# Layers 1 and 2 of a recommendation tower's MLP for two tiles at once, behind TensorE's inner loop

## The reference, cut to what matters

```python
x1 = einsum('bik,bjk,hij->bhk', e, e, W1) + b1      # e: [2048, 26, 32], gathered by ids
x2 = einsum('bik,bjk,hij->bhk', x1, e, W2) + b2     # 128 outputs each
z = concat([x1, x2], axis=1).sum(-1)                # [2048, 256]
h = concat([z, dense_ctx], axis=1)                  # [2048, 272]
h = maximum(h @ W_top1 + b_top1, 0)                 # "layer 1", 512 wide
h = maximum(h @ W_top2 + b_top2, 0)                 # "layer 2", 256 wide
y = h @ W_top3                                      # [2048, 1]
```

## Time and profile before

| | us |
|---|---|
| median of 3 runs | 509.12 (507.92 to 512.33) |
| the profiled execution | 510.54 |
| its span | 508.7 |
| mean granted TensorE clock | 0.993 |

### The profile page before, as it was taken

How to read it: one execution, slowest core, us unless ns; L and a number is a source line. 1 busy time by engine, 2 the same in 40 slices (tenths; PEclk the granted TensorE clock), 3 DMA queues, 4 the chain that set the end, 5 groups by cost and what they waited for, 6 DMA issues and landing times.

```text
span 508.7 us, 25085 instructions
## 1 busy us (share of the span) xinstructions
PE 479.8 (94%) x10786; PEld 461.8 (91%) x10786; DVE 377.7 (74%) x1095; ACT 253.5 (50%) x530; POOL 348.9 (69%) x274
## 2 busy tenths in 40 slices
PE   4998889969699999999999999999999999999998
PEld 4887879869699999999999999999999999999997
DVE  8698949495778788797969597959695968773202
ACT  8866835364525463636364545454454545455111
POOL 5888977467887888787878787878787887700000
PEclk9999999989989999999999999999999999999999
DMA  6620022120111102020202020202020200000000
GB/s 216 171 95 13 15 56 47 28 60 13 37 40 30 44 16 53 13 59 10 59 12 58 13 58 13 57 13 59 11 59 12 59 10 12 9 1 3 1 1 1
DMA packets 14001, 19.57 MB, mean 38 GB/s; under 512 B 5123, under 2 KB 11528, under 8 KB 13838
## 3 DMA queue, kind: packets, MB, share of 16 engines
q0 software_dynamic: 8512, 4.38, 8.1%
q1 hardware_dynamic: 5454, 14.73, 8.0%
HBM read 19.08 MB, written 0.01 MB: 38 GB/s over the span
## 4 chain that ended last, share of the span: by engine, by line
PE 78%; DVE 8%; issue 3%; ACT 3%; DMA 3%; POOL 2%; SPq 1%; ACTq 0%; DVEq 0%; POOLq 0%
PE psum L927 21%; PE psum L901 18%; PE psum L946 12%; PE psum L972 8%; PE psum L880 7%; PE psum L994 4%; PE psum L922 4%; DVE work L631 3%; POOL emb L389 2%; DMA onehot<-in_tbl 2%; PE psum L967 2%; DVE onehot L479 2%; DMA emb<-in_tbl,idx 1%; ACT t_area L742 1%; ACT v L706 1%
## 5 line engine op out<-in xcount | busy, mean ns | idle before, releaser
L389 POOL DMA_INDIRECT emb<-in_tbl,idx x266 | 348.1, 1309 | 95.0 <-issue 63.5
L742 ACT COPY t_area<-psum 128x432 f32<-128x432 f32 x256 | 124.5, 543 | 98.2 <-PE psum L901 71.3
L631 DVE TENSOR_TENSOR work<-embT 128x32 f32<-128x32 f32 (+12 forms) x416 | 129.3, 386 | 0.0
L927 PE MATMUL psum<-t_area,v 128*128 (+1 forms) x1088 | 124.1, 275 | 0.0
L927 PEld LDWEIGHTS psum<-t_area,v 128*128 128x128 f32 x1088 | 122.8, 192 | 0.0
L901 PE MATMUL psum<-diag,work 64*64 64x54 f32 (+1 forms) x6144 | 102.1, 216 | 4.8 <-ACT t_area L742 2.0
L901 PEld LDWEIGHTS psum<-diag,work 64*64 64x64 f32 (+1 forms) x6144 | 93.3, 126 | 11.5 <-issue 6.0
L719 ACT COPY diag<-embT 32x416 f32<-32x416 f32 x128 | 69.9, 546 | 20.6 <-DVE embT L613 19.1
L946 PE MATMUL psum<-table_parts,onehot 125*128 125x96 bf16 x1350 | 63.7, 208 | 4.1 <-DVE onehot L479 2.4
L946 PEld LDWEIGHTS psum<-table_parts,onehot 125*128 125x128 bf16 x1350 | 59.4, 99 | 6.5 <-DVE onehot L479 2.7
L880 PE MATMUL psum<-diag,work 128*64 128x108 f32 (+1 forms) x1024 | 51.5, 262 | 8.5 <-DVE work L631 6.6
(11 more groups left out here) (96 smaller groups left out, 447.1 us busy)
## 6 DMA issues: line engine op xcount, KB each, us to landing
ids_all<-in_short_ids SPq DMA_DIRECT2D x15, 625.0 KB
emb<-in_tbl,idx POOLq DMA_INDIRECT x266
t_area<-in_L_rec_W SPq DMA_DIRECT2D x1, 1664.0 KB, 8.5
work<-in_W_top SPq DMA_DIRECT2D x2, 512.0 KB, 12.2
onehot<-in_tbl SPq DMA_DIRECT2D x5, 156.2 KB
onehot<-in_tbl SPq DMA_DIRECT2D x5, 125.0 KB
t_area<-in_L_rec_W SPq DMA_DIRECT2D x1, 338.0 KB, 4.0
idx<-in_ids SPq DMA_DIRECT2D x1, 208.0 KB, 2.5
```

Of the source, the lines that this page charges most:

```text
L389: eng.indirect_dma_start(emb[n][:, f * K:(f + 1) * K], None, tables[f], bass.IndirectOffsetOnAxis(ap=idx[:, t * F + f:t * F + f + 1], axis=0),
L631: last = nc.vector.tensor_tensor(pairs[:, half, :, :, tri(r):tri(r) + r + 1], halves[:, g, :, 0:r + 1], halves[:, g, :, r:r + 1].broadcast ...
L742: nc.scalar.copy(dst, src).then_inc(t_out, 1)
L927: last = nc.tensor.matmul(z_ps(t)[:, NP:2 * NP], v[:, s, :], moments(slot), start=(a == 0), stop=(a == len(terms) - 1))
```

## The change

Layers 1 and 2 leave the inner loop's step and stand behind every second step (`layers(pair)`): layer 2 of the two tiles of a pair, then layer 1 of the next pair, for both tiles in one matmul of 256 columns. h1 of the four blocks of 128 outputs needs two PSUM banks then: blocks 0 and 1 are in bank 4, blocks 2 and 3 in bank 7, which rows part 0 and layer 2 of the pair's second tile use as well. ScalarE and VectorE move h1 in two halves per pair, and VectorE does `make_y` for two tiles together. Layer 1 of tiles 0 and 1 stands ahead of the loop. `pair` is i in round i of the loop, whose steps are 2i+3 and 2i+4.

```diff
+        def h2_ps(n):
+            return psum[:, 6 + n, 0:N2]
+        def h1_ps(half):
+            return psum[:, (4, 7)[half], :].rearrange("p (a b) -> p a b", b=2 * NP)
...
         def marks_in(t):
-            layers, cross = t >= 3, t != 1
-            return len(MARK_PHASES) + 2 + 2 * layers + len(MARK_TERMS) * cross
+            layer1, layer2, cross = t >= 2 and t % 2 == 0, t >= 4 and t % 2 == 0, t != 1
+            return len(MARK_PHASES) + 2 + 2 * layer1 + 2 * layer2 + len(MARK_TERMS) * cross
...
         (VectorE, tile)
                 make_pairs(t, n, (lambda: make_onehot(t + 1)) if not known or t + 1 < TILES else None)
                 if not known or t >= 2:
                     z_low(t - 2, n)
-                if not known or t >= 4:
-                    make_y(t - 4)
+                if n == 1 and (not known or t >= 5):
+                    for tile_of_pair in range(2):
+                        make_y(2 * i - 4 + tile_of_pair, tile_of_pair)
                 if not known or t >= 2:
                     pack(t - 1, 1 - n)
-                if not known or t >= 3:
-                    h1_low(t - 3)
+                if n == 1 and (not known or t >= 3):
+                    h1_low(i - 1)
...
         (ScalarE, step)
-                if not known or 3 <= t < TILES:
-                    h1_move(t - 3)
...
                 if not known or t >= 1:
-                    z_move(t - 1, 1 - n)
+                    z_move(t - 1, i - 1 + n, 1 - n)
+                if n == 0 and (not known or t >= 2):
+                    h1_move(i - 1)
...
         (TensorE, short_rows)
                     eng.wait_ge(rows_ready, t - 1)
-                    if part == 1 and not (isinstance(t, int) and t < 5):
-                        eng.wait_ge(y_ready, t - 3)
+                    if pair is not None:
+                        eng.wait_ge(y_ready if part else h1_lo_ready, 2 * pair + (1 if part else 3))
...
+            def layer1(pair):
+                if not (isinstance(pair, int) and pair == TILES // 2 - 1):
+                    eng.wait_ge(rows_ready, 2 * pair + 3)
+                eng.wait_ge(h1_lo_ready, 2 * pair + 1)
+                eng.wait_ge(z_out, 2 * pair + 2)
                 for a in range(N1 // NP):
+                    if a == 2:
+                        eng.wait_ge(y_ready, 2 * pair + 1)
+                    dst = h1_ps(a // 2)[:, a % 2, :]
                     cols = slice(a * NP, (a + 1) * NP)
+                    nc.tensor.matmul(dst, top1d[:, cols], denseT[:, bass.ts(pair, 2 * NP)], start=True, stop=False)
                     for top1, z in ((top1_hi, z_hi), (top1_lo, z_hi), (top1_hi, z_lo)):
                         if a == 0 and z is z_lo:
+                            eng.wait_ge(z_lo_ready, 2 * pair + 2)
...
-                t_units(t, 0)
-                if not known or t >= 3:
-                    layer1(t - 3, n)
-                t_units(t, 1)
-                if not known or t >= 3:
-                    layer2(t - 3)
-                if not known or t >= 2:
+                for half in range(2):
+                    t_units(t, half, pair)
+                if not isinstance(t, int) or t >= 2:
                     cin(t - 1, n)
+            def layers(pair):
+                for n in range(2):
+                    layer2(2 * pair + n, pair, n)
+                layer1(pair + 1)
...
+            layer1(0)
             with eng.Fori(0, (LOOP[1] - LOOP[0]) // 2) as i:
                 with eng.Fori(0, 2) as n:
-                    step(2 * i + n + LOOP[0], n)
+                    step(2 * i + n + LOOP[0], i, n)
+                layers(i)
```

More of the change, by code:

```diff
@@ L751, in z_move, with h1_move @@
                     .then_inc(z_out, 1)
[L753 to L759, removed]
+            def h1_move(pair):
+                if not (isinstance(pair, int) and pair < 1):
+                    eng.wait_ge(h2_full, 2 * pair)
+                for half in range(2):
+                    eng.wait_ge(h1_full, 2 * pair + half + 1)
+                    nc.scalar.activation(h1_hi[:, 2 * half:2 * half + 2, :], h1_ps(half), ACT.Relu).then_inc(h1_out, 1)
             def step(t, i, n):
@@ L792, in _ @@
                 step(t, t // 2, t % 2)
[L793 to L796, removed]
+            z_move(TILES - 1, TILES // 2 - 1, 1)
+            h1_move(TILES // 2 - 1)
         @block.tensor
@@ L861, in t_units @@
                             if v == at:
-                                short_rows(t + 1, part)
+                                short_rows(t + 1, part, pair)
                     if isinstance(t, int):
@@ L931, in cin, with short_rows @@
                 last.then_inc(z_full, 1)
-            def short_rows(t, part):
+            def short_rows(t, part, pair):
                 eng.wait_ge(onehot_ready, t)
@@ L973, in layer1, with layer2 @@
                                                     start=False, stop=(z is z_lo and s == 1))
-                    if a == 2:
-                        last.then_inc(progress, 1)
-                last.then_inc(h1_full, 1)
-            def layer2(t):
-                hi, lo = h1_parts(t)
-                eng.wait_ge(h1_out, t + 1)
-                if isinstance(t, int) and t == TILES - 1:
+                    last.then_inc(h1_full if a % 2 else progress, 1)
+            def layer2(t, pair, n):
+                eng.wait_ge(h1_out, 2 * pair + 2)
+                if isinstance(t, int) and t + 4 >= TILES:
@@ L993, in layer2 @@
                     for s in range(N1 // NP):
-                        last = nc.tensor.matmul(dst, h1[:, s * NP:(s + 1) * NP], top2[:, s, :], start=False,
-                                                stop=(h1 is lo and s == N1 // NP - 1))
-                        if h1 is lo and s == N1 // NP - 2:
+                        last = nc.tensor.matmul(dst, h1[:, s, n * NP:(n + 1) * NP], top2[:, s, :], start=False,
+                                                stop=(h1 is h1_lo and s == N1 // NP - 1))
@@ L997, in layer2, with step @@
+                        if h1 is h1_lo and s == N1 // NP - 2:
                             last.then_inc(progress, 1)
                 last.then_inc(h2_full, 1)
-            def step(t, n):
-                known = isinstance(t, int)
-                t_units(t, 0)
-                if not known or t >= 3:
-                    layer1(t - 3, n)
-                t_units(t, 1)
-                if not known or t >= 3:
-                    layer2(t - 3)
-                if not known or t >= 2:
+            def step(t, pair, n):
+                for half in range(2):
+                    t_units(t, half, pair)
+                if not isinstance(t, int) or t >= 2:
```

83 lines of the change are left out of this document (28 added, 55 removed).

## The result

| | before | after |
|---|---|---|
| median, us | 510.73 (507.92 to 512.87, 4 runs) | 544.87 (541.85 to 552.03, 4 runs) |
| ratio to before | | 1.0652, 95% interval 1.0563 to 1.0742 |
| the profiled execution | 510.54 | 541.85 |
| its span | 508.7 | 540.1 |
| mean granted TensorE clock | 0.993 | 0.949 |

The account below looks back on a forecast made before the run. GpSimd was taken to be as full as TensorE, behind its 94% busy share. Five pairs +26, start +6.2 and end -7.0 us, together +25, took the 508.7 us span to 534; median forecast 534, range 514 to 546.

Parts of the forecast that it names:

- GpSimd is the hidden limit: Gather queue: GpSimd as full as TensorE, needing 24.63 to 27.06 us per tile's gathers against TensorE's step of 26.40.
- G(8): End of a tile's last gather on GpSimd, here tile 8; claimed 2.99 us after the even step's phases 5 to 7 start.
- X(7): Moment TensorE starts phases 5 to 7 of the inner loop, here step 7; even step claimed to take 21.49 us.
- Rival (a): GpSimd is not the limit, gathers issue every 1.25 us; about 512 us; chance 0.10.
- The wait: TensorE at layer 1 waits for VectorE's z_low: 6.2 us per pair, 8.7 with two long gathers.
- The weight of 4 to 1: Odd tiles' gathers: one long gather weighed 4 to 1 against two, giving 58.0 us per pair against 52.8 before.
- After the wait: Rest of layer 1 to rows part 0: 6.6 us in place of 5.7, with 1.7 us lost to the clock.
- The saving: Layer 1 as 28 matmuls of 256 columns: 3.2 us less per pair, 25.7 us over 8 pairs.
- Rival (d): A 256-column layer 1 matmul costs two of 128, so nothing is saved; some 551 us; chance 0.02.
- (b): The layer 1 saving is kept whole: 484 us; chance 0.05.
- X(3): Loop's first start of phases 5 to 7: claimed at 158.5 in place of 152.33, +6.2 us.
- everything else has cover: Packs, second pairs, one-hot rows and ScalarE's h1 moves claimed to hold up nothing, but for 0.2 us left out.

Follow-up runs that it names:

- the idle matmuls: Changed kernel with 38 needless 256-column matmuls ahead of each layer 1 but the last, on the slow chip: 731.94 and 747.36 us, ratios 0.9808 and 1.0109.
- the fastest kernel: Changed kernel with z_low and y sums ahead of the second pairs, h1_low ahead of the packs, and gathers' marks four earlier: 496.6 us, 0.9743.
- before with earlier marks: Kernel before the change with AHEAD 2 in place of 6, on the slow chip: 737.81 and 718.82 us, ratios 0.9881 and 0.9738.
- ten gathers: Changed kernel with 10 gathers per tile in place of 16 from tile 2 on: 509.61 us, 1.0003.
- the gathers earlier: Changed kernel with AHEAD 2 in place of 6, so gathers wait for marks four earlier in TensorE's stream: 505.09 us, 0.9878.

## Why the prediction was right

The forecast was 534, and the median is 544.87: within the range of 514 to 546, but 1 us from its upper end. The direction and the mechanism came out as said; that the number still lay inside owes something to the width of the range. The sum was made for the span of one execution, which was to be 534 and is 540.1; that execution was the fastest of the four. Point by point:

- **GpSimd is the hidden limit.** Right, and the step most worth keeping. G(8) = X(7) + 2.99 as computed, 24.35 us for the next 16 gathers where 24.63 was taken, `z_lo` 16.35 behind the last one where 16.3 was taken. The rule that spoke against it, in the Trainium skill, SBUF — State Buffer, section "Who interferes with whom" (a tensor_tensor does not hold up descriptor generation; the skill calls this inferred), does not fit here either: the gather at 294.48 took 3.82 us, to 298.30, and from tile 5 on every long gather ends 0.8 to 1.1 us behind a block of pairs. But it is not as simple as the prediction has it ("it starts while VectorE forms the pairs (L631) and ends when those are done"), since not every gather in a block is held:

```profile
293.45 4.03 DVE L626 TENSOR_TENSOR work<-embT 128x32 f32<-128x32 f32 x13
308.73 4.09 DVE L626 TENSOR_TENSOR work<-embT 128x32 f32<-128x32 f32 x13
309.99 1.13 POOL L384 DMA_INDIRECT emb<-in_tbl,idx  x1 [0.30 <-issue]
```

  What picks out the one that is held no run shows. Rival (a), 512, which that rule would have backed, fell with the result.
- **The other signs.** TensorE's share is 87% for "about 85", X to X 22.0 and 35.9 for 21.5 and 36, and GpSimd is back to back in the even steps alone.
- **The wait.** Said: 6.2 with one long gather, 8.7 with two, longer at the start. Measured: 4.7 to 5.6 in the pairs with one, 7.5 where tile 13 had two, 7.9 at the start. The weight of 4 to 1 was met: of the five odd tiles that gate these waits, 5, 7, 9 and 11 had one long gather and 13 had two. That it was met exactly is luck: the prediction took it from how far G lies behind X, and G lay 2.99 behind X ahead of tile 13 too (397.71 for X(11) = 394.71). In the pair shown it is 0.9 shorter than the sum, 0.25 of it because `z_lo` came at X(7) + 43.69 where X + 43.94 was said, and 0.7 because TensorE came to it later (below): at 317.08, X(7) + 38.42, for 37.70.
- **After the wait.** 6.6 was taken from the wait's end to rows part 0 (4.9 of TensorE's own and 1.7 for the clock, with `h1_low` at 5.7 beneath it); 264.53 to 271.02 is 6.49, of which the rest of layer 1 at the lower clock is 4.50 for 2.8, and `h1_low` ended at 270.46, 5.93 behind the wait. The two limits overlap: by these numbers a full clock alone could have brought some 0.6 us, but the run meant to test it, with the idle matmuls, gave no number.
- **The saving.** 28 wide matmuls for 56 narrow ones: 0.120 apiece in the trace, 0.118 taken. Rival (d), that the wide ones cost double, is out; (b), the saving kept whole, is met by no run: the fastest kernel keeps 0.3 us of 3.2 per pair over all five, 1.0 over the last four.
- **What was mis-sized.** X(3) came at 160.9 for 158.5, the five pairs took 58.9 for 58.0 each, 4.7 us in all, and the tail 84.5 for 85.2: together the 6 us. In X(3) the excess lies behind rows part 0, which came as said (6.51 us behind the wait's end at 145.01): from there 9.38 us passed where 7.01 was taken, with stalls of TensorE of 1.33 and 0.23 us with no releaser in the profile. The 2.67 us for `z_hi` stand ahead of the wait for `z_lo` and cost nothing. The first pair took 59.9, 2.3 more than said for one long gather: a third such stall, 1.40 us, stands right behind X(3), and GpSimd waited 2.69 us for the mark behind it. No term of the sum covers these stalls. The next three pairs took 57.9, 57.9 and 58.1 for 57.55, the last one, with two long gathers, 60.9 for 60.0.
- **The missed term.** With layer 1 gone from between phases 3 and 4, TensorE comes to phase 4, and again to the last of phases 5 to 7, before ScalarE has emptied the bank. In the list of waits `t_area` L736 reads 7.2 us, 23 times. In before the same row read 2.0, 7 times. The even step has two such waits, 0.6 us, and is 22.00 in place of 21.49; this only shortens the wait for `z_lo` that follows. What costs is the one behind the wait: rows part 0 to the next X is 7.63 us (328.94 to 336.57) for 7.01. I had said "everything else has cover" and had checked VectorE's work and ScalarE's h1 moves for it, not the copies that layer 1 had been covering.
- **The tail** gained 7.7 us, 7.0 said, and TensorE lost only some 0.3 us there to `z_lo`. The reason is the one in the sum, VectorE's shorter turn: tile 15 makes no one-hot rows. Its gathers were as late as those of tile 9, 5.37 us behind X(14) (477.60) for 5.34, but `z_lo` followed 11.2 us behind the last of them in place of 16.35:

```profile
482.02 0.95 POOL L384 DMA_INDIRECT emb<-in_tbl,idx  x1 [0.30 <-issue]
```

The runs also answer what the prediction left as one mechanism: the ring of marks, gathers, VectorE's turn and `z_lo` has three places where it can be cut (the marks, the number of gathers, VectorE's order), and each cut alone brings back 31 to 40 us.

## What to carry to other kernels

A step moved next to its producer inherits the whole queue ahead of that producer: before you save matmuls on the busiest engine, follow the moved wait back through every engine in order, to the one that issues the loads. Progress marks that pace one engine by another are part of the schedule: when the marks' places move, count anew which load each one gates. And ask of every piece of work that is taken out what it was hiding, down to copies of 0.35 us, since they recur in every step.

## What the runs showed of the hardware

- **The clock's recovery differed between two streams.** After a wait of 5.25 us a stream of 256-column matmuls was back at the full level within 4.5 us (0.50, then 0.99 in the windows above). After a wait of 6.36 us a stream of 128-column matmuls in the same type stayed at 0.50 for all of its 11 us, to 295.64, and for over 4 us of the inner loop behind it (0.50 up to 300.00, then 0.72). At the lower level both stand 0.213 us apart, at the full one both some 0.12. Why the one brings the clock back and the other does not is not settled.
- **How long TensorE had waited does not tell whether the clock falls.** Behind a wait of 2.25 us it had fallen. With ten gathers, the windows over this wait and behind it:

```profile
248.00:252.00 4.00, 1.75 (x10) 1.66 (x10) 3.96 (x13) 0.00 (x0) 3.02 (x2) 0.85 0.06 17
252.00:256.00 4.00, 4.00 (x104) 3.87 (x107) 3.31 (x8) 1.31 (x3) 1.55 (x2) 0.73 0.03 4
```

  What was left of layer 1 took 4.45 us (250.34 to 254.79), hardly less than behind twice the wait. In the same run the granted clock stayed at 1.00 behind a wait of 2.28 us (197.48), and with the gathers earlier behind one of 2.65 us, where the rest of the layer took 2.92 (350.31 to 353.23):

```profile
352.00:356.00 4.00, 3.91 (x154) 3.65 (x153) 3.28 (x8) 2.31 (x6) 2.91 (x4) 1.00 0.07 12
```

- **Narrow fp32r matmuls cost what wide ones do.** The Trainium skill, TensorE: Matmul & The Clock Gate, section "Back-to-back issue gap", gives about 81 ns for a matmul of 128 columns with its weight load in a sustained stream. The trace shows 117 ns for layer 1 before, so the measured number decides, and it is what makes twice the columns free.
- **The same kernel can take half as long again on another chip.** Before took 747 and 754 us there for 510, and in the profiles of that chip TensorE has stalls with no releaser in the inner loop: 74.2 us for before with earlier marks, 57.4 for the fastest kernel, 28.9 for the one with 84 gathers fewer (190 in place of 274 instructions on GpSimd). That TensorE was short of instructions, and that the gathers have a part in it, is a guess; nothing here shows the path.
